# Moving the early input's Hadamard work and the queries' turn to other gaps of an attention pipeline

## Chip, cores and metric

One core of one Trainium2 chip. The metric is the device time of one launch in microseconds (us), as the median of several runs.

## What is computed

The reference is one gated block on 16 sequences of 128 tokens with 512 features, all in fp32:

```python
x = x + tanh(g_xattn[0]) * attention(layernorm(x), ctx, ctx)     # 32 query heads, 8 key/value heads, D = 16
x = x + tanh(g_ffn[0]) * ffn(layernorm(x))

def h_bitlinear(x, w):
    xq = act_quant(fwht(x))          # Hadamard transform, then 8 bits by the row's absolute maximum
    wq = weight_quant(w)             # ternary by the mean absolute weight
    return einsum('bsh,oh->bso', xq, wq)

ffn = h_bitlinear(silu(h_bitlinear(x, w_gate)) * h_bitlinear(x, w_up), w_down)   # 512 -> 2048 -> 512
```

`attention` is a softmax over 128 context positions of the scores divided by 4; keys and values are both the context.

## The kernel before

All 16 sequences (called batches) stay in SBUF. The kernel has two large stages: attention over batches 0 to 15, and then the feed-forward part over four units of four batches. The engines run programs of their own, written out by hand, and meet through counting semaphores; nothing is scheduled for them. What a function such as `step(b)` says for an engine is the order in which that engine works. The change is in the first stage, in `step(b)` of TensorE (`block.tensor`) and of ScalarE (`block.scalar`).

In step b of the attention stage TensorE computes four **quarters**. Quarter (b, j) makes two things side by side: the transposed scores of two groups of heads of batch b (L602 and L627, two PSUM banks, which ScalarE turns into weights with `exp`, L1014), and the *row products* of a quarter seven ahead (L619), that is, scores of batch b+1 or b+2 in the other layout, of which VectorE takes the maxima over the context (`maximum`, L1279, two instructions a quarter). The row products of one quarter go to the two banks that those of the quarter before had, so that they wait for the semaphore `max_done`. Between the quarters lie:

- `weigh(n, kvh)` (L662): the weights times the values of one half of the heads, into bank 6 (`O_BANK`); ScalarE's `copy_out` (L1022) takes it out and counts `oev_done`
- `turn_out(n, kvh)` (L679): that half turned back into rows by tokens, into bank 7 (`T_BANK`); VectorE's `finish` (L1290, L1292) divides by the sums and counts `fin_done`, and GpSimd adds it to x
- `turn_queries(b + 3)` (L716): the normalised queries of a later batch turned, into bank 6; ScalarE's `copy_queries` (L1036) takes them out and counts `qt_done`
- the early input work. The first four batches' attention is complete early, so their input to the feed-forward part is prepared inside the attention stage: `early_turn` in steps 7, 9, 11 and 13 (L725, taken out by `feed_first`, L1110), `early_had` in steps 8, 10, 12 and 14 (L735, the Hadamard product, taken out by `copy_had`, L1072), `early_second` in steps 9, 11, 13 and 15 (L742, taken out at L1104). In the kernel before, all of these use bank 7.

VectorE's `step(b)` is, in this order: the maxima of the first quarter; integers of the early input (L1345, steps 9, 11, 13); batch statistics of batch b+4 (L1264 to L1268, up to step 11); the second quarter's maxima; `finish(b - 1, 0)`; the third quarter's maxima; in steps 8, 10, 12 and 14 `early_peak` (L1327 to L1332, the absolute maximum of the copied Hadamard product); the fourth quarter's maxima; `finish(b - 1, 1)`; `early_round` (L1338); and at the end of steps 5, 7, 9 and 11 the statistics of an early input (L1242 to L1246), ahead of the next step's maxima. GpSimd shifts weights (L466) and works on the early input in between (L491 to L497). Between the second quarter and the third of step b the sign of weights runs on ScalarE (L1052).

In the kernel before, TensorE's row in a step is: quarter 0, `weigh(b-1, 1)`, early turn or early Hadamard product, quarter 1, `turn_out(b-1, 0)`, `turn_queries(b+3)`, quarter 2, `weigh(b, 0)`, `early_second`, quarter 3, `turn_out(b-1, 1)`. Steps 14 and 15 are in `last_steps()`, which the change leaves alone.

## Time and profile before

| | |
|---|---|
| median of 3 runs | 474.78 us (474.51 to 475.0) |
| profiled execution, its time | 474.27 us |
| its span | 472.5 us |
| TensorE busy | 458.6 us |
| VectorE busy | 391.0 us |
| ScalarE busy | 292.8 us |
| GpSimd busy | 211.8 us |

The profile is of one execution. Busy time of TensorE is modelled from pipelined matmuls, which can lie over one another: two matmuls on different rows of the array run side by side and show as two rows that start together. So the table says which engine is loaded, and the timeline, with the starts of the pieces, says where a piece is held.

### The profile page before, as it was taken

The page shows a single profiled execution, that of the slowest core. Times are in us where ns is not written, and L with a number is a line of the kernel's source. Part 1 is how long each engine was busy: PE and PEld are TensorE (multiplying, and loading weights), DVE is VectorE, ACT ScalarE, POOL GpSimd, SP SyncE. Part 2 cuts the span into 40 slices and gives each one's busy share as a digit, 9 for nine tenths or more (in the row PEclk, how much of TensorE's full clock was granted, in tenths as well). Part 3 has the DMA queues.
Part 4 walks back from the last instruction along what each step waited for, and adds up shares of the span by engine and source line. Part 5 has one row for each costly group of instructions (what it writes and reads, how often), then busy time and mean ns, then how long its engine had stood idle before and what let it go on. Part 6 is the DMA issues. An engine that isn't in the chain of part 4 may idle for free.

```text
span 472.5 us, 9016 instructions
## 1 busy us (share of the span) xinstructions
PE 458.6 (97%) x3130; PEld 298.9 (63%) x3130; DVE 391.0 (83%) x745; ACT 292.8 (62%) x465; POOL 211.8 (45%) x314
## 2 busy tenths in 40 slices
PE   8999999999999989999999999999999999999997
PEld 7665656566656534468944469864468874479664
DVE  4889998888977759859998967999895999889892
ACT  4478886667777688877647417643616663647460
POOL 4245455989888464655006734202916300930000
PEclk9999999999999999999999999999999999999999
DMA  7999120121014050000100651100361110153086
GB/s 223 323 348 347 45 53 12 24 58 25 13 22 112 13 166 36 1 1 13 24 11 1 112 135 32 22 11 0 67 141 61 24 24 0 28 92 61 1 140 217
DMA packets 68183, 35.90 MB, mean 76 GB/s; under 512 B 50288, under 2 KB 62960, under 8 KB 68144
## 3 DMA queue, kind: packets, MB, share of 16 engines
q1 hardware_dynamic: 67728, 34.61, 28.8%
q10 hardware_dynamic: 416, 0.79, 0.5%
q8 instruction: 22, 0.36, 0.3%
q14 instruction: 17, 0.14, 0.1%
HBM read 19.26 MB, written 4.19 MB: 50 GB/s over the span
## 4 chain that ended last, share of the span: by engine, by line
PE 70%; DVE 13%; issue 7%; ACT 4%; POOL 2%; DMA 1%; SPq 1%; DVEq 0%; POOLq 0%; ACTq 0%
PE ps L863 15%; PE ps L619 10%; PE ps L917 9%; PE ps L602 8%; PE ps L662 6%; PE ps L940 6%; PE ps L679 3%; PE ps L929 2%; PE ps L931 2%; PE ps L806 2%; DVE wst L1447 2%; ACT wst L1052 2%; DVE y_split L1422 2%; PE ps L716 1%; PE ps L627 1%
## 5 line engine op out<-in xcount | busy, mean ns | idle before, releaser
L863 PE MATMUL ps<-wst 128*128 128x512 bf16 x512 | 113.0, 379 | 2.1 <-DVE wst L1442 2.1
L1279 DVE TENSOR_REDUCE reg<-ps 128x4 f32<-128x512 f32 x128 | 81.9, 684 | 24.7 <-PE ps L619 24.0
L863 PEld LDWEIGHTS ps<-wst 128*128 128x128 bf16 x512 | 49.0, 98 | 62.2 <-DVE wst L1442 4.2
L619 PE MATMUL ps<-reg 32*128 32x256 f32 x512 | 86.7, 400 | 0.9 <-DMA reg<-in_k_t 0.5
L1014 ACT ACTIVATE reg<-ps 128x1024 f32<-128x1024 f32 x64 | 65.6, 1025 | 32.8 <-PE ps L627 32.5
L564 POOL TENSOR_TENSOR reg_rest<-reg_rest,z_sc 128x1024 f32<-128x1024 f32 x24 | 47.3, 2012 | 84.6 <-DVE z_sc L1484 84.6
L1146 ACT ACTIVATE wst<-wst 128x512 f32<-128x512 f32 x64 | 40.0, 627 | 51.8 <-DVE wst L1442 51.5
L917 PE MATMUL ps<-had_f,wst 128*128 128x128 f32 x512 | 67.1, 276 | 1.1 <-DVE wst L1447 1.1
L917 PEld LDWEIGHTS ps<-had_f,wst 128*128 128x128 f32 x512 | 64.1, 191 | 4.4 <-DVE wst L1447 1.8
L602 PE MATMUL ps<-reg 32*128 32x512 f32 x232 | 65.2, 639 | 0.0
L619 PEld LDWEIGHTS ps<-reg 32*128 32x128 f32 x512 | 58.7, 184 | 5.8 <-ACT reg L1036 1.0
L1176 ACT CAST y_split<-ps 128x512 fp32r<-128x512 f32 x64 | 37.4, 585 | 35.8 <-PE ps L917 35.8
L1422 DVE TENSOR_TENSOR y_split<-ps,y_split 128x512 fp32r<-128x512 f32 x64 | 43.4, 683 | 15.0 <-ACT y_split L1176 15.0
L1442 DVE TENSOR_TENSOR wst<-ps,wst 128x512 f32<-128x512 f32 x64 | 43.5, 680 | 8.2 <-PE ps L863 8.2
L1447 DVE TENSOR_TENSOR wst<-ps,wst 128x512 f32<-128x512 f32 x64 | 43.4, 678 | 1.4 <-ACT wst L1146 1.3
L940 PE MATMUL ps<-wst,reg_rest 128*128 128x512 bf16 x192 | 42.8, 380 | 0.0
L1185 ACT COPY reg_rest<-ps 128x512 f32<-128x512 f32 x64 | 37.8, 591 | 2.1 <-PE ps L931 2.1
L459 POOL TENSOR_TENSOR x_all<-x_all,reg 128x256 f32<-128x256 f32 x32 | 23.9, 746 | 32.9 <-DVE reg L1292 32.8
L1461 DVE TENSOR_REDUCE mz<-reg_rest 128x8 f32<-128x1024 f32 (+1 forms) x33 | 38.3, 1171 | 0.0
L940 PEld LDWEIGHTS ps<-wst,reg_rest 128*128 128x128 bf16 x192 | 27.4, 144 | 13.9 <-issue 0.5
L662 PE MATMUL ps<-reg 128*32 128x512 f32 x256 | 34.1, 605 | 0.1
L929 PE MATMUL ps<-y_split,had_r 128*128 128x512 f32 x64 | 30.6, 478 | 0.0
(168 smaller groups left out, 738.1 us busy)
## 6 DMA issues: line engine op xcount, KB each, us to landing
wst<-in_w SPq DMA_DIRECT2D x16, 512.0 KB, 8.6
reg<-in_w SPq DMA_DIRECT2D x8, 512.0 KB, 5.6
out<-x_all SPq DMA_DIRECT2D x16, 256.0 KB, 2.1
x_all<-in_x SPq DMA_DIRECT2D x3, 1024.0 KB, 9.5
reg<-in_k_t SPq DMA_DIRECT2D x32, 32.0 KB, 2.4
reg<-in_v SPq DMA_DIRECT2D x4, 256.0 KB, 4.1
x_all<-in_x ACTq DMA_DIRECT2D x1, 512.0 KB, 4.8
reg_rest<-reg SPq DMA_TRANSPOSE x20, 3.0
```

The lines of the kernel that those rows point to most:

```text
L564: pool.tensor_tensor(z, z, sc, ALU.mult).then_inc(sem("z_scaled"), 1)
L602: pe.matmul(ps[:, bank + m, :], kpad[b // CHUNK % 2][strip(i), b % CHUNK, a, :], q_t[b % 4][strip(i), :], start=True, stop=False)
L619: last = pe.matmul(ps[:, row_banks(r) + m, 256 * g:256 * g + 256], q_t[n % 4][strip(i), P * h:P * h + P], kpad[n // CHUNK % 2][strip(i), n ...
L662: last = pe.matmul(O_BANK[SLOT * l:SLOT * l + SLOT, :], v_pad[n // CHUNK % 2][:, n % CHUNK, 4 * kvh + l, :], probs[:, 4 * kvh + l, :], sta ...
L863: last = pe.matmul(ps[:, banks[ob % n], :], tern_gu[:, ob // 2, m, j, P * (ob % 2):P * (ob % 2) + P], q1_t[:, j, :], start=(j == 0), stop= ...
L917: last = pe.matmul(ps[:, Y_BANKS[s % 3], P * k:P * k + P], X[:, 4 * s + k, :, :].rearrange("p c t -> p (c t)"), had_f[:, :], start=True, s ...
L940: last = pe.matmul(ps[:, bank, :], q2.rearrange("p g (t c) -> p c (g t)", c=NC)[:, c, P * tb:P * tb + P], tern_d[:, c, :], start=(c == 0), ...
L1014: act.activation(probs[:, 2 * j:2 * j + 2, :], ps[:, bank:bank + 2, :], ACT.Exp, scale=D ** -0.5).then_inc(sem("exp_done"), 1)
L1279: dve.tensor_reduce(neg_max[n % 2][:, g:g + 2, i + m, :], ps[:, row_banks(r) + m, :].rearrange("p (g a t) -> p g a t", g=2, a=2), AX_X, AL ...
L1422: dve.tensor_tensor(y_low[s % RING], ps[:, Y_BANKS[s % 3], :], y_high[s % RING].bitcast(F32), ALU.subtract).then_inc(sem("y_low"), 1)
L1442: dve.tensor_tensor(gs[ob % GS], ps[:, G_BANKS[ob % 2], :], s_row, ALU.mult).then_inc(sem("gs_done"), 1)
L1447: dve.tensor_tensor(X[:, :, ob, :], ps[:, U_BANKS[ob % 3], :].rearrange("p (g t) -> p g t", g=NG), gs[ob % GS].rearrange("p (g t) -> p g t ...
```

## The change

In steps 7 to 13 (`EARLY`) the early turn or the early Hadamard product moves from behind quarter 0 to behind quarter 1 and `turn_out(b-1, 0)`, and goes into bank 6 instead of bank 7. Bank 6 is free there only when `copy_out(b-1, 1)` is through (`oev_done`), and `weigh(b, 0)`, which writes bank 6 next, waits for ScalarE's copy. The queries' turn, which has bank 6 too, moves from its place behind quarter 1 to the end of the step, behind quarter 3 and `turn_out(b-1, 1)`; it waits for `copy_out(b, 0)`, and `weigh(b, 1)` waits for its copy. ScalarE's copies are moved in the same way. In step 14 the Hadamard product keeps its place and bank. The orders of VectorE, GpSimd and the DMA queues are the same.

```diff
--- before.py
+++ after.py
@@ -236,12 +236,17 @@
         FIRST_DMA = 5
         SECOND_UNIT = {13: (0, 1), 15: (2, 3)}
         FRONTS = {5: 0, 7: 1, 9: 2, 11: 3}
+        EARLY = range(7, 14)
         G_PLACE = 5
         ROUND_ACT = {9: 0, 11: 1}
         G_BANKS = (0, 2)
         U_BANKS = (1, 3, 6)
         T_BANK = ps[:, 7, :]
         O_BANK = ps[:, 6, :]
+
+        def had_bank(b):
+
+            return O_BANK if b in EARLY else T_BANK
 
         block = ctx.enter_context(nc.Block())
 
@@ -652,7 +657,11 @@
                     pe.wait_ge(sem("v_set"), n // CHUNK + 1)
                 pe.wait_ge(sem("exp_done"), QUARTERS * n + 2 * kvh + 2)
                 reach(pe, sem("oev_done"), 2 * n + kvh)
-                if kvh == 0 and exists(n + 3):
+                if kvh == 0 and n in EARLY_HAD and n in EARLY:
+                    pe.wait_ge(sem("f_hc"), EARLY_HAD[n] + 1)
+                if kvh == 0 and n in EARLY_TURN:
+                    pe.wait_ge(sem("f_xt"), EARLY_TURN[n] + 1)
+                if kvh == (1 if n in EARLY else 0) and exists(n + 3):
                     pe.wait_ge(sem("qt_done"), n + 4)
                 if kvh == 1 and n + 1 < FIRST_DMA:
                     pe.wait_ge(sem("mt_done"), n + 2)
@@ -669,12 +678,10 @@
                     return
                 pe.wait_ge(sem("oev_done"), 2 * n + kvh + 1)
                 reach(pe, sem("fin_done"), 2 * n + kvh)
-                if kvh == 0 and n + 1 in EARLY_HAD:
+                if kvh == 0 and n + 1 in EARLY_HAD and n + 1 not in EARLY:
                     pe.wait_ge(sem("f_hc"), EARLY_HAD[n + 1] + 1)
                 if kvh == 1 and n + 1 in EARLY_SECOND:
                     pe.wait_ge(sem("f_sg"), EARLY_SECOND[n + 1] + 1)
-                if kvh == 0 and n + 1 in EARLY_TURN:
-                    pe.wait_ge(sem("f_xt"), EARLY_TURN[n + 1] + 1)
                 for g in range(G):
                     last = pe.transpose(T_BANK[:, P * g:P * g + P], o_t[kvh][:, P * g:P * g + P], ident_f[:, :])
                 last.then_inc(sem("to_done"), 1)
@@ -711,7 +718,7 @@
                 elif n == 2:
                     pe.wait_ge(sem("qt_done"), 2)
                 elif n > 3:
-                    pe.wait_ge(sem("oev_done"), 2 * (n - 3))
+                    pe.wait_ge(sem("oev_done"), 2 * (n - 3) + (1 if n - 3 in EARLY else 0))
                 for j in range(NJ):
                     last = pe.transpose(O_BANK[:, P * j:P * j + P], q_norm[n % 2][:, P * j:P * j + P], ident_f[:, :])
                 last.then_inc(sem("tq_done"), 1)
@@ -720,9 +727,9 @@
 
                 tb = EARLY_TURN[b]
                 pe.wait_ge(sem("f_b2"), 2 * tb + 2)
-                pe.wait_ge(sem("fin_done"), 2 * b - 2)
+                pe.wait_ge(sem("oev_done"), 2 * b)
                 for j in range(NJ):
-                    last = pe.transpose(T_BANK[:, P * j:P * j + P], xn_first[tb][:, P * j:P * j + P], ident_f[:, :])
+                    last = pe.transpose(O_BANK[:, P * j:P * j + P], xn_first[tb][:, P * j:P * j + P], ident_f[:, :])
                 last.then_inc(sem("f_t1"), 1)
 
             def early_had(b):
@@ -730,9 +737,12 @@
                 if tb == 0:
                     pe.wait_ge(sem("const_in"), 16 * 5)
                 pe.wait_ge(sem("f_xt"), tb + 1)
-                pe.wait_ge(sem("fin_done"), 2 * b - 2)
+                if b in EARLY:
+                    pe.wait_ge(sem("oev_done"), 2 * b)
+                else:
+                    pe.wait_ge(sem("fin_done"), 2 * b - 2)
                 for j in range(NJ):
-                    last = pe.matmul(T_BANK[:, P * j:P * j + P], xn_t[:, P * j:P * j + P], had_f[:, :], start=True, stop=True)
+                    last = pe.matmul(had_bank(b)[:, P * j:P * j + P], xn_t[:, P * j:P * j + P], had_f[:, :], start=True, stop=True)
                 last.then_inc(sem("f_h"), 1)
 
             def early_second(b):
@@ -771,19 +781,22 @@
             def step(b):
                 quarter(b, 0)
                 weigh(b - 1, 1)
+                quarter(b, 1)
+                turn_out(b - 1, 0)
                 if b in EARLY_HAD:
                     early_had(b)
                 if b in EARLY_TURN:
                     early_turn(b)
-                quarter(b, 1)
-                turn_out(b - 1, 0)
-                turn_queries(b + 3)
+                if b not in EARLY:
+                    turn_queries(b + 3)
                 quarter(b, 2)
                 weigh(b, 0)
                 if b in EARLY_SECOND:
                     early_second(b)
                 quarter(b, 3)
                 turn_out(b - 1, 1)
+                if b in EARLY:
+                    turn_queries(b + 3)
                 turn_max(b + 1)
 
             def down_sum():
@@ -1066,20 +1079,24 @@
                 act.wait_ge(sem("const_in"), 16 * 5)
                 act.copy(had16_r.rearrange("p (t c) -> p c t", c=NC), xn_t[:, 0:P].rearrange("p (c t) -> p c t", c=NC)).then_inc(sem("had16_set"), 1)
 
-            def copy_had(tb):
+            def copy_had(b):
+                tb = EARLY_HAD[b]
                 act.wait_ge(sem("f_h"), tb + 1)
                 reach(act, sem("f_qf"), tb)
-                act.copy(had_out, T_BANK).then_inc(sem("f_hc"), 1)
+                act.copy(had_out, had_bank(b)).then_inc(sem("f_hc"), 1)
 
             def step(b):
                 exp(b, 0)
                 copy_out(b - 1, 1)
-                if b in EARLY_HAD:
-                    copy_had(EARLY_HAD[b])
+                if b in EARLY_HAD and b not in EARLY:
+                    copy_had(b)
+                exp(b, 1)
+                if b in EARLY_HAD and b in EARLY:
+                    copy_had(b)
                 if b in EARLY_TURN:
                     feed_first(EARLY_TURN[b])
-                exp(b, 1)
-                copy_queries(b + 3)
+                if b not in EARLY:
+                    copy_queries(b + 3)
                 halves = ABS_ACT.get(b, ())
                 for h in halves[0:1]:
                     absolute(h)
@@ -1090,6 +1107,8 @@
                 if b in EARLY_SECOND:
                     feed_second(EARLY_SECOND[b])
                 exp(b, 3)
+                if b in EARLY:
+                    copy_queries(b + 3)
                 copy_max(b + 1)
                 for h in halves[1:]:
                     absolute(h)
@@ -1107,7 +1126,7 @@
                 act.wait_ge(sem("f_t1"), tb + 1)
                 reach(act, sem("f_h"), tb)
                 act.wait_ge(sem("had16_set"), 1)
-                act.copy(xn_t, T_BANK).then_inc(sem("f_xt"), 1)
+                act.copy(xn_t, O_BANK).then_inc(sem("f_xt"), 1)
 
             act.wait_ge(sem("mhalf_set"), 3)
             normalise_q(0)
```

TensorE's row in step 8, from the end of quarter 0. L602, L619 and L627 are a quarter, L662 weighs, L735 is the Hadamard product, L679 `turn_out`, L716 `turn_queries`. Before:

```order
L627 MATMUL ps<-reg 128x512 x2
L662 MATMUL ps<-reg 32x512 x4
L735 MATMUL ps<-had_f,wst 128x128 x4
L602 MATMUL ps<-reg 128x512 x2
L619 MATMUL ps<-reg 128x256 x4
L627 MATMUL ps<-reg 128x512 x2
L679 MATMUL ps<-ident_f,reg 128x128 x4
L716 MATMUL ps<-ident_f,reg 128x128 x4
L602 MATMUL ps<-reg 128x512 x2
```

After (L607, L624, L632 are a quarter, L671 weighs, L745 is the Hadamard product, L686 `turn_out`):

```order
L632 MATMUL ps<-reg 128x512 x2
L671 MATMUL ps<-reg 32x512 x4
L607 MATMUL ps<-reg 128x512 x2
L624 MATMUL ps<-reg 128x256 x4
L632 MATMUL ps<-reg 128x512 x2
L686 MATMUL ps<-ident_f,reg 128x128 x4
L745 MATMUL ps<-had_f,wst 128x128 x4
L607 MATMUL ps<-reg 128x512 x2
```

The Hadamard product has gone from behind the weighing to behind `turn_out`, where the queries' turn stood; between quarters 0 and 1 only the weighing is left.

The same engine from quarter 3 of step 8 to the first matmuls of step 9, before:

```order
L602 MATMUL ps<-reg 128x512 x2
L619 MATMUL ps<-reg 128x256 x4
L627 MATMUL ps<-reg 128x512 x2
L679 MATMUL ps<-ident_f,reg 128x128 x4
L602 MATMUL ps<-reg 128x512 x2
```

After (L723 is `turn_queries`):

```order
L607 MATMUL ps<-reg 128x512 x2
L624 MATMUL ps<-reg 128x256 x4
L632 MATMUL ps<-reg 128x512 x2
L686 MATMUL ps<-ident_f,reg 128x128 x4
L723 MATMUL ps<-ident_f,reg 128x128 x4
L607 MATMUL ps<-reg 128x512 x2
```

The queries' turn now stands between quarter 3 and the next step's quarter 0.

ScalarE in step 8, from the exponential of quarter 0 on: L1014 is an exponential, L1022 `copy_out`, L1072 `copy_had`, L1036 `copy_queries`, L1052 a sign of weights. Before (the first row also holds the last exponential of step 7):

```order
L1014 ACTIVATE reg<-ps 128x1024 x2
L1022 COPY reg<-ps 128x512
L1072 COPY wst<-ps 128x512
L1014 ACTIVATE reg<-ps 128x1024
L1036 COPY reg<-ps 128x512
L1052 ACTIVATE wst<-wst,magics 128x1024
L1014 ACTIVATE reg<-ps 128x1024
L1022 COPY reg<-ps 128x512
L1014 ACTIVATE reg<-ps 128x1024
```

After (L1027 an exponential, L1035 `copy_out`, L1086 `copy_had`, L1065 a sign, L1049 `copy_queries`):

```order
L1027 ACTIVATE reg<-ps 128x1024
L1035 COPY reg<-ps 128x512
L1027 ACTIVATE reg<-ps 128x1024
L1086 COPY wst<-ps 128x512
L1065 ACTIVATE wst<-wst,magics 128x1024
L1027 ACTIVATE reg<-ps 128x1024
L1035 COPY reg<-ps 128x512
L1027 ACTIVATE reg<-ps 128x1024
L1049 COPY reg<-ps 128x512
```

The copy of the Hadamard product goes behind the second exponential, and the queries' copy behind the fourth.

## Rows read from the trace of the kernel before

**Rows 1.** The page's first part, TensorE: busy us (share of the span), instructions.
```profile
PE 458.6 (97%) x3130; PEld 298.9 (63%) x3130; DVE 391.0 (83%) x745; ACT 292.8 (62%) x465; POOL 211.8 (45%) x314
```

**Rows 2.** Timeline of TensorE, batch 12: start us, us, instruction, count.
```profile
137.28 0.66 PE L679 MATMUL ps<-ident_f,reg 128*128 128x128 f32 x4
...
137.87 0.70 PE L602 MATMUL ps<-reg 32*128 32x512 f32 x2
...
139.62 1.07 PE L662 MATMUL ps<-reg 128*32 128x512 f32 x8
...
140.61 1.16 PE L735 MATMUL ps<-had_f,wst 128*128 128x128 f32 x8
...
141.70 0.70 PE L602 MATMUL ps<-reg 32*128 32x512 f32 x2
...
142.97 0.66 PE L679 MATMUL ps<-ident_f,reg 128*128 128x128 f32 x4
...
144.00 0.70 PE L602 MATMUL ps<-reg 32*128 32x512 f32 x2
...
145.38 1.06 PE L662 MATMUL ps<-reg 128*32 128x512 f32 x8
...
147.65 0.66 PE L679 MATMUL ps<-ident_f,reg 128*128 128x128 f32 x4
```

**Rows 3.** Timeline of VectorE, batch 12, its maxima; idle time before them in brackets.
```profile
137.22 1.29 DVE L1279 TENSOR_REDUCE reg<-ps 128x4 f32<-128x512 f32 x2 [1.50 <-PE ps L619]
...
140.18 1.28 DVE L1279 TENSOR_REDUCE reg<-ps 128x4 f32<-128x512 f32 x2
...
142.98 1.29 DVE L1279 TENSOR_REDUCE reg<-ps 128x4 f32<-128x512 f32 x2 [1.52 <-PE ps L619]
...
145.21 1.29 DVE L1279 TENSOR_REDUCE reg<-ps 128x4 f32<-128x512 f32 x2 [0.26 <-PE ps L619]
```

**Rows 4.** Timeline of TensorE and then of VectorE, batch 6.
```profile
78.34 1.07 PE L662 MATMUL ps<-reg 128*32 128x512 f32 x8
...
81.30 0.66 PE L679 MATMUL ps<-ident_f,reg 128*128 128x128 f32 x4
...
78.91 1.28 DVE L1279 TENSOR_REDUCE reg<-ps 128x4 f32<-128x512 f32 x2
80.11 0.68 DVE L1264 BATCH_NORM_STATS2 st<-x_all 128x6 f32<-128x512 f32 x1
...
81.12 1.29 DVE L1279 TENSOR_REDUCE reg<-ps 128x4 f32<-128x512 f32 x2
```

**Rows 5.** Timeline of TensorE and then of VectorE, batch 13.
```profile
149.98 1.06 PE L662 MATMUL ps<-reg 128*32 128x512 f32 x8
...
152.84 0.66 PE L679 MATMUL ps<-ident_f,reg 128*128 128x128 f32 x4
...
155.24 1.06 PE L662 MATMUL ps<-reg 128*32 128x512 f32 x8
...
157.93 0.66 PE L679 MATMUL ps<-ident_f,reg 128*128 128x128 f32 x4
...
149.93 1.27 DVE L1279 TENSOR_REDUCE reg<-ps 128x4 f32<-128x512 f32 x2
151.13 0.41 DVE L1345 TENSOR_SCALAR q_b<-wst 128x512 bf16<-128x512 f32 x1
...
152.84 1.29 DVE L1279 TENSOR_REDUCE reg<-ps 128x4 f32<-128x512 f32 x2 [1.30 <-PE ps L619]
```

**Rows 6.** Timeline of VectorE, batch 11, the first quarter's maxima.
```profile
129.41 1.27 DVE L1279 TENSOR_REDUCE reg<-ps 128x4 f32<-128x512 f32 x2
```

**Rows 7.** Timeline of ScalarE, batch 12, the copy of the Hadamard product.
```profile
141.81 0.59 ACT L1072 COPY wst<-ps 128x512 f32<-128x512 f32 x1 [0.47 <-PE ps L735]
```

**Rows 8.** Timeline of VectorE and then of GpSimd, end of batch 10.
```profile
126.60 0.45 DVE L1332 TENSOR_SCALAR f_max<-wsc,f_max 128x2 f32<-128x2 f32 x1
...
125.90 1.12 POOL L466 TENSOR_SCALAR wst<-wst,w_inv 128x1024 f32<-128x1024 f32 x1
```

## The prediction

> **What bounds the kernel now.** The page's first part comes first: TensorE is busy for 97% of the span [rows 1]. That share alone says little here, since a matmul that waits in a queue behind a semaphore does not show as idle. So I read next the timeline of TensorE in one batch of the stage that the change touches, batch 12 [rows 2], and beside it VectorE's maxima [rows 3]. In the rows I take as the end of a quarter the start of what follows it on TensorE, since TensorE works in order.
>
> The reader is to see how long each piece takes. The second quarter runs from 141.70 to 142.97, 1.27 us. The first runs from 137.87 to 139.62, 1.75 us, and the third from 144.00 to 145.38, 1.38 us. All three hold the same matmuls, so 0.48 us of the first and 0.11 of the third are waiting. The wait is for VectorE: a quarter's row products (L619) may not write their two banks before the two maxima (L1279) of the quarter before have read them. The maxima of the fourth quarter begin at 137.22 and the next quarter ends at 139.62, 2.40 later; those of the second begin at 142.98 and the third ends at 145.38, again 2.40 later [rows 2, 3]. In batch 6 they begin at 78.91 and the quarter ends at 81.30, 2.39 later [rows 4]; in batch 13 from 152.84 to 155.24, 2.40 [rows 5]. So this stage has one rule, in numbers of this trace: **a quarter ends at the later of (its start + 1.27) and (start of the former quarter's maxima + 2.40)**. What TensorE does between two quarters is free up to about 1.1 us, and dear beyond it.
>
> The other durations: weighing 0.99 (139.62 to 140.61), the Hadamard product 1.09 (140.61 to 141.70), turning a half of the output 0.59 (137.28 to 137.87), and with the queries' turn 1.03 (142.97 to 144.00), so the queries' turn is 0.44 [rows 2]. The early input's turn (L725) lies in batch 13 between 149.98 and 152.84 with a weighing and a quarter: 2.86 - 0.99 - 1.27 = 0.60 [rows 5].
>
> **The change, part by part.** No operation is added or removed; bank 6 stands in for bank 7 and two pieces of TensorE's row change place. Seen from TensorE alone this fills gaps: the queries' turn goes to where 0.48 us are waited, the early work away from where weighing already fills 0.99. What it is worth is decided by when VectorE starts its maxima, and VectorE's own order is not touched.
>
> *The queries' turn before the first quarter.* In batch 12's place the first quarter would start at 137.28 + 1.03 = 138.31 and end at 139.58 unhindered; the maxima give 137.22 + 2.40 = 139.62. It ends at 139.62, as now. The 0.44 us are hidden in the wait, but nothing comes earlier.
>
> *Even batches 8, 10, 12 (Hadamard product).* Behind the first quarter only the weighing is left, so the second could start at 140.61 and end at 141.88. But VectorE starts the first quarter's maxima only at 140.18, because in batches 7, 9 and 11 the statistics of an early input (L1242 to L1246) stand ahead of them. 140.18 + 2.40 = 142.58. Batch 6 shows this very case, for the statistics of batch 5 stand ahead of it and it has no early work between its first two quarters: its second quarter begins after 78.34 + 0.99 = 79.33 and ends at 81.30, 1.97 us, a wait of 0.70 [rows 4]. So the second quarter comes 0.39 earlier than now (142.97), not 1.09. Then follow 0.59 + 1.09 and the third quarter: 142.58 + 1.68 + 1.27 = 145.53, against 145.38 now. The second quarter's maxima don't bind it: even where batch statistics follow the first maxima (batches 8 and 10), VectorE is free at 140.18 + 1.20 + 1.01 = 142.39, and 2.40 more is 144.79. (1.20 from 78.91 to 80.11, 1.01 from 80.11 to 81.12 [rows 4].) The third quarter's maxima start 1.21 after it, as from 144.00 to 145.21 [rows 2, 3]: 144.26 + 1.21 = 145.47, and the fourth ends at the later of 145.53 + 0.99 + 1.27 = 147.79 and 145.47 + 2.40 = 147.87. Now it ends at 147.65. **A Hadamard batch gets 0.22 us longer**: the product now lies where it is no longer a cover for VectorE's lateness. Three of them: +0.66.
>
> *Batch 13 (turn, last one).* First quarter at 149.98 as now; its maxima start at 149.93, so the second ends at 149.93 + 2.40 = 152.33 (unhindered 152.24) against 152.84. Then 0.59 + 0.60 + 1.27 gives 154.79 (VectorE's integers, 0.41 from 151.13, are done long before and do not bind). From there to the batch's end 2.69 as now (155.24 to 157.93), 157.48: 0.45 shorter [rows 5].
>
> *Batches 9 and 11.* They have batch statistics as well. In batch 11 the first maxima start at 129.41 [rows 6], so the second quarter ends at 131.81, and VectorE comes to the second maxima at 129.41 + 1.20 + 0.41 + 1.01 = 132.03. The third quarter: unhindered 131.81 + 0.59 + 0.60 + 1.27 = 134.27, by the maxima 134.43; plus 2.69 is 137.12, against 137.28 [rows 2]. 0.16 shorter each, 0.32 for both. Batch 7 has no Hadamard batch ahead and the weights' scales on VectorE; I take 0.1, between nothing and batch 11's 0.16.
>
> *New waits, costed at nothing.* Weighing (b, 0) now waits for ScalarE's copy out of bank 6. In batch 12 the product would end at 142.58 + 0.59 + 1.09 = 144.26; the copy starts 0.11 behind it (141.70 to 141.81) and takes 0.59 [rows 7], so it is done at 144.96, and the weighing is due at 145.53: 0.57 us of cover. After the turn in batch 13 the cover is the same to 0.02. The queries' copy is done 1.03 + 0.11 + 0.59 = 1.73 behind the fourth quarter, the weighing (b, 1) due 2.34 behind it: 0.61 of cover. If a cover were gone, its batch would lose what is missing; behind these copies on ScalarE stand a sign or an exponential, whose result TensorE asks for two quarters later.
>
> The sum: +0.66 - 0.45 - 0.32 - 0.10 = **-0.21 us**. The profiled execution took 474.27 (span 472.5), and 474.06 would follow; its time lies 0.51 below the median of the runs, 474.78, and I put the same difference against that: 474.6. Behind batch 13 everything moves along, and batches 14 and 15 are as they were.
>
> **The rivals.** Measurement tells 0.2%, 0.95 us, from no change.
> - *TensorE's gaps count in full.* If the maxima followed TensorE at once, the queries' turn would save 1.75 - 1.38 = 0.37 in front of six batches, and the early work 0.11 in six third quarters and 155.24 - 152.84 - 0.59 - 1.27 = 0.54 in batch 13: 2.22 + 0.66 + 0.54 = 3.4 us, 471.4. For it speaks that each of these gaps is in the rows; against it batch 6, and that the first quarter's maxima at 140.18 don't depend on TensorE. 8 in 100. A share of it, over 0.95, because VectorE comes to its maxima earlier in most batches: 473.5, 6 in 100.
> - *Even batches break even.* If only their 0.66 were wrong, the result is -0.87, 473.9, still no change that can be told: 8 in 100.
> - *VectorE is held by GpSimd.* Ahead of the fourth quarter's maxima in a Hadamard batch stands a small product (L1332). In batch 10 it runs from 126.60 to 127.05 while GpSimd shifts weights from 125.90 to 127.02 [rows 8]: it ends when that does, and the maxima behind it, on which the next batch's first quarter depends, come late. The change moves VectorE against GpSimd. If it now meets the start of such an instruction it is held for its whole 1.12 us instead of 0.45, 0.67 a batch; with its neighbour L1338 held likewise twice that. Three batches give 2.0 to 4.0, less 0.2: 476.6 to 478.6. It decides from (0.95 + 0.21) / 3 = 0.39 a batch. GpSimd's order follows VectorE's though, and the moves are of 0.2 us. 6 in 100.
> - *A new wait binds.* Were ScalarE late by 0.57 plus 0.2 in each of seven batches (a sign ahead of the copy would do it, and none stands there), +1.2 net, 476.0. 3 in 100.
>
> The Trainium skill's page "SBUF — State Buffer" (section "Who interferes with whom") says that VectorE and GpSimd share one port pair as an exclusive lock, which a scalar product out of SBUF can take and which a reduction never needs. The trace agrees for L1332, which ended 0.03 from the end of GpSimd's instruction; no row here shows maxima held. By that rule the sum stays and only the third rival lives.
>
> **How the numbers follow.** Forecast 0.69, its own range 474.0 to 475.1, from 0.05 to 0.1 of error in each of seven batches. With "even batches break even" 0.77 lie within 0.2%; faster 0.14 (0.08 + 0.06); slower 0.09 (0.06 + 0.03). The range, which may leave out 2 in 10, goes to 473.7 below and 475.5 above.
>
> **What the changed profile would show.** Right: between the end of the fourth quarter and the end of the next first quarter still 2.34 us; a second quarter of about 1.97 us in batches 8, 10 and 12; third quarters of 1.27 in the even batches; the batches' lengths up by 0.2 in the even ones and down by 0.1 to 0.5 in the odd ones; no wait of the weighing on ScalarE's copies. Wrong: second quarters of 1.3 us in the even batches (first rival), the small product L1332 longer than 0.5 us (third), or the weighing starting over 0.1 behind the third quarter's last matmul (fourth).

## The result: faster, and by far more than forecast

The changed kernel takes 472.91 us (median of 6 runs, 472.81 to 473.67) against 474.70 us for the kernel before (6 runs, 474.29 to 475.0). The ratio is 0.9968 with a 95% interval of 0.9957 to 0.9978. That is a gain of 1.0 to 2.0 us where 0.2 was forecast, and outside the range. Its profiled execution took 472.94 us, 1.33 less than that of before. The kernel before took 474.36 to 474.46 us (medians of 7 to 21 executions) beside the later experiments, so the gain may well be nearer to 1.5 us than to the 1.8 between the two medians above. One execution of e6 ran at a granted clock of 0.982 (481.89 us) and is left out of its ratio; all others of the experiments ran at 0.999 or 1.000.

The page's head and first part, after:

```profile
span 471.1 us, 8996 instructions
## 1 busy us (share of the span) xinstructions
PE 455.3 (97%) x3110; PEld 299.1 (63%) x3130; DVE 390.4 (83%) x745; ACT 292.2 (62%) x465; POOL 211.2 (45%) x314
```

The span is 1.4 us shorter (472.5 before). TensorE's share of it is the 97% of [rows 1]: waits in its queue don't show as idle. The stretches that follow are batches 7 to 13, each from the end of its predecessor's fourth quarter to the end of its own, by the starts of `turn_out` on TensorE. Columns: stretch and its length, then busy time and count of TensorE, its weight loads, VectorE, ScalarE and GpSimd, the granted clock (1.00 is the 2.4 GHz level), DMA share and GB/s. Before:

```profile
85.93:95.73 9.80, 9.80 (x93) 6.04 (x91) 7.94 (x19) 6.63 (x9) 8.96 (x17) 1.00 0.06 13
95.73:106.09 10.36, 10.36 (x95) 6.48 (x93) 9.24 (x22) 7.23 (x9) 8.06 (x15) 1.00 0.26 66
106.09:116.49 10.40, 10.40 (x93) 6.18 (x91) 8.38 (x19) 8.40 (x11) 9.81 (x18) 1.00 0.14 28
116.49:126.86 10.37, 10.37 (x95) 6.48 (x93) 9.26 (x22) 7.22 (x9) 8.52 (x16) 1.00 0.06 13
126.86:137.28 10.42, 10.42 (x93) 6.21 (x90) 8.39 (x19) 8.40 (x11) 9.83 (x19) 1.00 0.12 27
137.28:147.65 10.37, 10.37 (x95) 6.48 (x93) 8.32 (x20) 7.23 (x9) 8.07 (x15) 1.00 0.43 115
147.65:157.93 10.28, 10.28 (x90) 5.99 (x87) 7.08 (x15) 7.98 (x10) 8.19 (x14) 1.00 0.13 27
```

After:

```profile
86.09:95.54 9.45, 9.45 (x88) 5.96 (x86) 7.82 (x19) 6.06 (x8) 8.61 (x17) 1.00 0.06 14
95.54:105.85 10.31, 10.31 (x94) 6.59 (x92) 9.07 (x22) 7.21 (x9) 8.28 (x15) 1.00 0.25 66
105.85:116.01 10.16, 10.16 (x92) 6.28 (x90) 8.26 (x19) 8.33 (x11) 9.56 (x18) 1.00 0.14 29
116.01:126.39 10.38, 10.38 (x94) 6.63 (x92) 9.13 (x22) 7.22 (x9) 8.71 (x16) 1.00 0.06 13
126.39:136.56 10.17, 10.17 (x93) 6.28 (x91) 8.27 (x19) 8.33 (x11) 9.58 (x19) 1.00 0.13 27
136.56:146.94 10.38, 10.38 (x95) 6.63 (x93) 8.28 (x20) 7.22 (x9) 8.88 (x16) 1.00 0.48 115
146.94:156.59 9.65, 9.65 (x92) 5.89 (x90) 7.12 (x15) 8.17 (x11) 7.51 (x13) 1.00 0.13 29
```

| batch | 7 | 8 | 9 | 10 | 11 | 12 | 13 | sum |
|---|---|---|---|---|---|---|---|---|
| forecast | -0.10 | +0.22 | -0.16 | +0.22 | -0.16 | +0.22 | -0.45 | -0.21 |
| measured | -0.35 | -0.05 | -0.24 | +0.01 | -0.25 | +0.01 | -0.63 | -1.50 |

The whole gain lies in these seven batches. (In the execution of after, batch 7 begins 0.16 us later, and what follows passes the gain on: 1.34 at the end of batch 13, 1.4 in the span.) Every batch is better than forecast. The three with the Hadamard product miss by 0.21 to 0.27 each, 0.69 together, and the four others by 0.60. TensorE's timeline of batch 12, after, beside [rows 2]:

```profile
136.56 0.66 PE L686 MATMUL ps<-ident_f,reg 128*128 128x128 f32 x4
...
137.58 0.70 PE L607 MATMUL ps<-reg 32*128 32x512 f32 x2
...
138.89 1.06 PE L671 MATMUL ps<-reg 128*32 128x512 f32 x8
...
139.89 0.70 PE L607 MATMUL ps<-reg 32*128 32x512 f32 x2
...
141.85 0.66 PE L686 MATMUL ps<-ident_f,reg 128*128 128x128 f32 x4
...
142.34 1.06 PE L745 MATMUL ps<-had_f,wst 128*128 128x128 f32 x8
...
143.33 0.70 PE L607 MATMUL ps<-reg 32*128 32x512 f32 x2
...
144.60 1.07 PE L671 MATMUL ps<-reg 128*32 128x512 f32 x8
...
146.94 0.66 PE L686 MATMUL ps<-ident_f,reg 128*128 128x128 f32 x4
```

And VectorE's maxima of the fourth quarter of batch 11 and the first of batch 12, beside [rows 3]:

```profile
136.49 1.29 DVE L1298 TENSOR_REDUCE reg<-ps 128x4 f32<-128x512 f32 x2 [1.69 <-PE ps L624]
...
139.46 1.28 DVE L1298 TENSOR_REDUCE reg<-ps 128x4 f32<-128x512 f32 x2
```

The first quarter ends 138.89 - 136.56 = 2.33 behind the batch's start, as forecast (2.34). The first maxima begin 2.90 behind it, as before, and the second quarter ends at 141.85, 5.29 behind (forecast 5.30), 2.39 behind the start of those maxima: it takes 1.96 us, 0.69 of them waiting. So far each number is the forecast's. Then `turn_out` and the Hadamard product take 143.33 - 141.85 = **1.48** us. The forecast had added 0.59 and 1.09, 1.68, from their durations in [rows 2]. `turn_out` starts 0.49 ahead of the product, and the product 0.99 ahead of the quarter. That 0.20 is what the batch misses.

### The profile page after: what moved, and what is told of

It is laid out like the page before. It is cut to its first block, busy times and chain, and to the rows that moved or that the text cites. A ratio compares the mean times of both kernels' runs of the same rounds, so it can differ in the third digit from the quotient of the medians.

```text
span 471.1 us, 8996 instructions
## 1 busy us (share of the span) xinstructions
PE 455.3 (97%) x3110; PEld 299.1 (63%) x3130; DVE 390.4 (83%) x745; ACT 292.2 (62%) x465; POOL 211.2 (45%) x314
## 4 chain that ended last, share of the span: by engine, by line
PE 70%; DVE 13%; issue 8%; ACT 4%; POOL 2%; DMA 1%; SPq 1%; DVEq 0%; POOLq 0%; ACTq 0%
PE ps L876 15%; PE ps L624 10%; PE ps L930 9%; PE ps L607 7%; PE ps L671 6%; PE ps L953 6%; PE ps L686 4%; PE ps L942 2%; PE ps L944 2%; PE ps L819 2%; DVE wst L1466 2%; DVE y_split L1441 2%; ACT wst L1065 2%; PE ps L632 2%; PE ps L723 1%
## 5 line engine op out<-in xcount | busy, mean ns | idle before, releaser
L876 PE MATMUL ps<-wst 128*128 128x512 bf16 x499 | 111.7, 379 | 3.3 <-DVE wst L1461 2.1
L624 PE MATMUL ps<-reg 32*128 32x256 f32 x512 | 87.0, 399 | 1.2 <-DMA reg<-in_k_t 0.7
L1027 ACT ACTIVATE reg<-ps 128x1024 f32<-128x1024 f32 x64 | 65.5, 1024 | 32.0 <-PE ps L632 31.8
L607 PE MATMUL ps<-reg 32*128 32x512 f32 x232 | 65.2, 639 | 0.0
L624 PEld LDWEIGHTS ps<-reg 32*128 32x128 f32 x512 | 59.2, 184 | 6.2 <-ACT reg L1049 1.3
L671 PE MATMUL ps<-reg 128*32 128x512 f32 x256 | 34.1, 605 | 0.1
L607 PEld LDWEIGHTS ps<-reg 32*128 32x128 f32 x232 | 17.5, 183 | 24.9 <-issue 23.5
```

Of the source, the lines that this page charges most:

```text
L607: pe.matmul(ps[:, bank + m, :], kpad[b // CHUNK % 2][strip(i), b % CHUNK, a, :], q_t[b % 4][strip(i), :], start=True, stop=False)
L624: last = pe.matmul(ps[:, row_banks(r) + m, 256 * g:256 * g + 256], q_t[n % 4][strip(i), P * h:P * h + P], kpad[n // CHUNK % 2][strip(i), n ...
L671: last = pe.matmul(O_BANK[SLOT * l:SLOT * l + SLOT, :], v_pad[n // CHUNK % 2][:, n % CHUNK, 4 * kvh + l, :], probs[:, 4 * kvh + l, :], sta ...
L876: last = pe.matmul(ps[:, banks[ob % n], :], tern_gu[:, ob // 2, m, j, P * (ob % 2):P * (ob % 2) + P], q1_t[:, j, :], start=(j == 0), stop= ...
L1027: act.activation(probs[:, 2 * j:2 * j + 2, :], ps[:, bank:bank + 2, :], ACT.Exp, scale=D ** -0.5).then_inc(sem("exp_done"), 1)
```

## The experiments

**Theory.** TensorE works in blocks: quarters and weighings use 32-row or 32-column tiles of its array (32\*128, 128\*32 in the rows), transposes and Hadamard products the full 128\*128. A block of full-array matmuls between tiled ones costs some 0.15 to 0.20 us beyond its matmuls, once. Four transposes add 0.43 to 0.44, four products 0.89. In the kernel before, the early work was a block of its own; now it shares one with `turn_out`. **Rival theory:** the pieces are shorter at the new place for another reason (bank, neighbours that are lighter). A second question is what holds VectorE in front of the maxima.

### e1: the change in the odd batches only

```diff
-        EARLY = range(7, 14)
+        EARLY = (7, 9, 11, 13)
...
                 weigh(b - 1, 1)
+                if b in EARLY_HAD and b not in EARLY:
+                    early_had(b)
```

> The change only in the odd batches 7, 9, 11 and 13; batches 8, 10 and 12 keep the Hadamard product behind the weighing, in bank 7, and the queries' turn behind the second quarter. By the prediction's sum (a moved Hadamard product costs 0.22 us a batch) this must be 0.66 us faster than the changed kernel: 472.3, even batches of 10.37 us as before the change. By the theory formed on the trace of after (a block of full-array matmuls that joins another saves the 0.20 us which it costs to stand alone, which pays for the 0.22) the even batches are worth nothing either way: 472.9, and again batches of 10.3 to 10.4 us.

Measured 473.08 us, ratio to before 0.9973 (0.9963 to 0.9983), against 0.9968 for the full change. Batches 8, 10 and 12 are 10.32, 10.36 and 10.36 us, batches 9, 11 and 13 10.14, 10.20 and 9.70, as in after. The prediction's sum would have had 472.3, a ratio of 0.995, which lies outside the interval. So in even batches the change is worth nothing either way: what VectorE's lateness costs without its cover (0.22) is what the shared block gives back (0.20).

### e2: a small tiled matmul between `turn_out` and the early work

```diff
                 turn_out(b - 1, 0)
+                if b in EARLY:
+                    pe.wait_ge(sem("oev_done"), 2 * b)
+                    pe.matmul(O_BANK[:, 0:8], kpad[b // CHUNK % 2][strip(0), b % CHUNK, 0, :],
+                              q_t[b % 4][strip(0), 0:8], start=True, stop=True)
                 if b in EARLY_HAD:
                     early_had(b)
```

> The changed kernel with one tiny matmul on a 32-row tile (8 columns, its result is overwritten) between turn_out and the early work in batches 7 to 13, so that the early work no longer follows full-array matmuls directly. In after, turn_out and the product take 1.48 us in batch 12 (from 141.85 to 143.33), turn_out and the early turn 1.02. Theory 'each change between tiled and full-array matmuls costs about 0.1 us': 1.68 or more and 1.2 or more, even batches 10.5 to 10.6 us instead of 10.3 to 10.4. Rival 'the pieces are shorter because of the other bank or the other place': 1.50 and 1.05, batches unchanged.

TensorE in batch 12 of this kernel (L686 `turn_out`, L788 the small matmul, L745 the product):

```profile
143.76 0.66 PE L686 MATMUL ps<-ident_f,reg 128*128 128x128 f32 x4
144.35 0.38 PE L788 MATMUL ps<-reg 32*128 32x8 f32 x2
144.66 1.16 PE L745 MATMUL ps<-had_f,wst 128*128 128x128 f32 x8
145.75 0.70 PE L607 MATMUL ps<-reg 32*128 32x512 f32 x2
```

`turn_out` is back at 0.59 and the product at 1.09 (144.66 to 145.75), the very durations that they have apart in the kernel before, though bank and place are the new ones. The small matmul takes 0.31 itself, so the even batches take 10.83 to 10.88 us, more than the 10.5 to 10.6 expected. The kernel took 475.66 us in one run. The rival theory falls: bank and place are those of the changed kernel. A small full-array matmul in the same place was not run, so e2 alone leaves open whether any matmul between would do it. But in the changed kernel transposes with other weights and another bank stand directly ahead of the product, and the 0.20 is gone; so neither a change of weights nor one of bank costs it.

### e7: the Hadamard product twice, in the kernel before

```diff
-                for j in range(NJ):
+                for j in [*range(NJ), *range(NJ)]:
                     last = pe.matmul(T_BANK[:, P * j:P * j + P], xn_t
```

> The kernel before with the early Hadamard product issued twice in a row at its old place (same operands, same result). Alone it takes 1.09 us between a weighing and a quarter. Theory 'a block of full-array matmuls costs about 0.2 us for standing alone, and the product 0.89': the two take 1.98 us. Rival 'the product takes 1.09 at this place': 2.18.

```profile
99.21 2.05 PE L735 MATMUL ps<-had_f,wst 128*128 128x128 f32 x16
101.19 0.70 PE L602 MATMUL ps<-reg 32*128 32x512 f32 x2
```

16 instead of 8 rows, and 1.98 us: the second product cost 0.89. With 1.09 for the first, standing alone costs 0.20. (477.57 us, one run.)

The traces also say at which end of a block it is paid. In the changed kernel `turn_out` takes 0.59 us ahead of a quarter and 0.49 ahead of another full-array piece: 0.10 for leaving. The product takes 1.09 behind a weighing and 0.99 behind `turn_out`, 0.10 for entering; the early turn takes 0.59 and 0.53, 0.06 for entering. Weighings and quarters don't pay: in every order that was run an unhindered quarter takes 1.27 to 1.28 us and a weighing 0.99 to 1.00, whatever stands beside them. But a weighing (128\*32) and a quarter (32\*128) always alternate with each other or with full-array pieces, so what a change between these two tiled forms costs was not seen.

### e6: only the queries' turn moved

```diff
                 turn_out(b - 1, 0)
-                turn_queries(b + 3)
+                if b not in EARLY:
+                    turn_queries(b + 3)
...
                 turn_out(b - 1, 1)
+                if b in EARLY:
+                    turn_queries(b + 3)
```

The waits for bank 6 and ScalarE's copy move with it, as in the change.

> The kernel before with only the queries' turn moved to the end of steps 7 to 13; the early work stays behind the weighing in bank 7. By the rule that a quarter ends no earlier than 2.40 us behind the start of the former quarter's maxima, the queries' turn was hidden in neither place: the third quarters and the first quarters both end where they did, batches stay 10.36 to 10.42 us, 474.5. By the rival 'TensorE's gaps count in full' the first quarters shrink by 0.37 us in six batches: 472.3.

474.35 us, ratio 0.9998 (0.9989 to 1.0008). In batch 10 the third quarter starts 0.44 us earlier, behind `turn_out` alone:

```profile
121.90 0.66 PE L680 MATMUL ps<-ident_f,reg 128*128 128x128 f32 x4
122.49 0.70 PE L603 MATMUL ps<-reg 32*128 32x512 f32 x2
...
124.30 1.07 PE L663 MATMUL ps<-reg 128*32 128x512 f32 x8
```

It still ends 2.40 behind the start of the second quarter's maxima (121.90 on VectorE, L1286). The rule on the maxima holds in both places, and the rival "TensorE's gaps count in full" is out.

### e3 and e4: the early input's statistics at another place of VectorE's order

```diff
                 maximum(b + 2, 1)
+                if b in FRONTS:
+                    reach(dve, sem("f_ap"), FRONTS[b])
+                    statistics(Index(None, FRONTS[b]), ("f_bn", "f_mv", "f_ve"), 2)
...
-                if b in FRONTS:
-                    reach(dve, sem("f_ap"), FRONTS[b])
-                    statistics(Index(None, FRONTS[b]), ("f_bn", "f_mv", "f_ve"), 2)
```

e3 does this in the changed kernel, e4 in the one before.

> The changed kernel with the early input's statistics on VectorE (end of steps 5, 7, 9, 11) done between the third and fourth quarter's maxima of the same step instead of ahead of the next step's first maxima. Theory 'in even batches the second quarter waits 0.70 us for maxima that these statistics make late': the second quarters of batches 6, 8, 10 and 12 fall from 1.95 to 1.3 us, batch 6 gets 0.56 shorter, 8, 10 and 12 about 0.6 each, 2.4 in all, 470.5 us. Rival 'TensorE waits there for something else (ScalarE's exponential, GpSimd's maxima)': nothing, 472.9. If the statistics only make the fourth quarter's maxima late instead, odd batches get up to 1 us longer and the time is 472.5 to 473.5.

> The same move of the statistics in the kernel before the change. If the early Hadamard product behind the first weighing covers VectorE's lateness, as the prediction has it, only batch 6 gains, 0.56 us: 474.1. If the lateness costs time there as well, batches 8, 10 and 12 gain too, up to 2 us, 472.7.

**e3** took 471.36 us, ratio 0.9936 (0.992 to 0.9953); once more beside e9 (below), 471.54 and 0.9937. The second quarter of batch 10 is down from 1.96 to 1.30 us, on TensorE:

```profile
118.76 0.70 PE L607 MATMUL ps<-reg 32*128 32x512 f32 x2
...
120.06 0.66 PE L686 MATMUL ps<-ident_f,reg 128*128 128x128 f32 x4
```

Batches 8, 10 and 12 are 9.71 us each, 0.60 to 0.67 shorter, and batch 6 went from 9.92 to 9.27. That is 2.6 us, where 2.4 were expected. But batches 7, 9, 11 and 13 got longer, 9.78, 10.41, 10.48 and 9.83, 1.07 us together, which the expectation had not counted. GpSimd's shift of weights (L471), VectorE's product of scales (L1351) and the maxima behind it, in batch 8 of e3:

```profile
104.25 1.13 POOL L471 TENSOR_SCALAR wst<-wst,w_inv 128x1024 f32<-128x1024 f32 x1
...
104.81 0.59 DVE L1351 TENSOR_SCALAR f_max<-wsc,f_max 128x2 f32<-128x2 f32 x1
...
105.30 1.27 DVE L1298 TENSOR_REDUCE reg<-ps 128x4 f32<-128x512 f32 x2
```

A product of two columns takes 0.59 us and ends at 105.40; GpSimd's instruction ends at 105.38. The maxima begin 0.28 behind the end of the fourth quarter (105.02) instead of ahead of it. In batch 8 of each of these kernels the product ends within 0.03 us of a GpSimd instruction's end: 0.42 us in the kernel before, 0.35 in after, 0.59 in e3, 0.76 in e4, where it came behind the start of the instruction after the shift, L491, and waited for that one. From after to e3 the products ahead of batches 9, 11 and 13 got longer by 0.24, 0.31 and 0.18 us, and in batch 7 the product of the weights' scales (L1377, also 128x2) went from 0.36 to 0.63: 1.00 of the 1.07. **e4** took 474.53 us, ratio 0.9999 (0.9989 to 1.0009), not the 474.1 expected: batch 6 gained 0.64, and batches 9 and 11 lost 0.35 and 0.33, ahead of which the products took 0.34 and 0.30 us longer. The even ones stayed at 10.36 us, so the old place of the product did cover the statistics, as the prediction said.

### e5 and e8: the product of scales behind the maxima

```diff
-                dve.tensor_scalar(f_max[:, 4:6], wsc[:, 0:2], f_max[:, 1:2], C_E, ALU.mult, ALU.mult
-                                  ).then_inc(sem("f_c"), 1)
             def early_round(tb):
-                dve.wait_ge(sem("f_c"), 4 * tb + 4)
+                dve.wait_ge(sem("f_c"), 4 * tb + 3)
+                dve.tensor_scalar(f_max[:, 4:6], wsc[:, 0:2], f_max[:, 1:2], C_E, ALU.mult, ALU.mult
+                                  ).then_inc(sem("f_c"), 1)
```

e5 is this on e3, e8 on the changed kernel.

> The kernel of e3 with VectorE's small product of scales (L1351, 128x2) moved from ahead of the fourth quarter's maxima to behind them and behind finish, at the start of early_round. In e3 it ran 0.59 and 0.66 us in batches 8 and 10, each time until GpSimd's shift of weights ended, and batches 9 and 11 were 10.41 and 10.48 us instead of the 10.16 of after. Theory 'VectorE was held by GpSimd in front of the maxima on which the next first quarter waits': the maxima begin at the end of the fourth quarter again, batches 9, 11 and 13 get 0.2 to 0.3 us shorter each, 470.7. Rival 'odd batches are longer because the statistics now stand between the third and fourth quarter's maxima': no change, 471.4.

> The changed kernel with only the small product of scales moved behind the fourth quarter's maxima. In after it ran 0.35 us in batches 8 and 10 and ended with GpSimd's shift of weights, and the maxima began 0.04 us behind the end of the fourth quarter, 0.10 later than they could. Theory of the port: up to 0.1 us in two batches, 472.8, which a time can't tell from none but the profile can: the maxima of the fourth quarter of batches 8 and 10 begin 0.05 ahead of its end. Rival: the maxima are late because of the peak's own reduction, and nothing moves.

Both expectations failed. e5 took 471.88 us (0.9946, 0.9932 to 0.9959), not 470.7, and e8 474.27 (0.9998, 0.9989 to 1.0008), 1.4 over after where at most 0.1 was at stake. The maxima of the fourth quarter do begin on time. But the product now meets the next GpSimd instruction and holds back `early_round` (L1357), which then meets the one after. Batch 8 into 9 of e5, L501 and L502 being GpSimd's butterflies:

```profile
106.48 0.78 DVE L1355 TENSOR_SCALAR f_max<-wsc,f_max 128x2 f32<-128x2 f32 x1
...
106.51 0.73 POOL L501 TENSOR_TENSOR wst<-wst 128x256 f32<-128x256 f32 x1
...
107.17 1.03 DVE L1357 TENSOR_SCALAR wst<-wst,f_max 128x512 f32<-128x512 f32 x1
...
107.19 0.74 POOL L502 TENSOR_TENSOR wst<-wst 128x256 f32<-128x256 f32 x1
...
108.13 1.27 DVE L1298 TENSOR_REDUCE reg<-ps 128x4 f32<-128x512 f32 x2
```

The next first maxima, at 108.13, are 3.40 behind the end of the batch (104.73), against 2.50 in after. Batch 9 is 11.03 us in e5, and batches 9 and 11 are 10.82 each in e8, 0.65 over after. So the mechanism was right and the place wrong: held instructions line up.

### e9 and e11: the product of scales on ScalarE

```diff
+            def scales_act(tb):
+                act.wait_ge(sem("wsce_done"), 1)
+                act.wait_ge(sem("f_c"), 4 * tb + 3)
+                act.activation(f_max[:, 4:6], wsc_e[:, :], ACT.Copy, scale=f_max[:, 1:2]).then_inc(sem("f_c"), 1)
```

Both are built on e3. ScalarE calls this behind the queries' copy, and VectorE's product is taken out of `early_peak`. In e9 VectorE makes `wsc_e` (the weights' scales times a constant) in batch 7, in e11 ScalarE does in batch 8.

> The kernel of e3 with the small product of scales off VectorE: ScalarE makes it behind the queries' copy (one copy with a scale, from the weights' scales times a constant, which VectorE makes once in batch 7). Nothing of two columns stands ahead of the fourth quarter's maxima, or ahead of early_round as in e5. Theory of the port: maxima of the fourth quarter at its end minus 0.05 in batches 8, 10 and 12, and early_round, if it meets no GpSimd instruction, 0.5 to 0.6 us: batches 9 and 11 of about 10.1 to 10.2 us instead of 10.4 and 10.5, 470.7. If early_round itself is held (1.0 us, as in e5), nothing is won over e3, 471.4 to 471.9.

> The kernel of e3 once more, beside e9 on the same chip, so that the two can be compared: 471.4, 3.0 us under the kernel before.

> The kernel of e9 with the weights' scales times the constant also made by ScalarE, in batch 8. In e9 VectorE made them in batch 7 ahead of the first maxima, which began 1.40 us behind the statistics of the weights instead of 0.94 in e3, and batch 7 was 10.25 us instead of 9.78, while batches 9 and 11 were 9.87. Theory: every small product out of SBUF ahead of maxima can be held by GpSimd, so batch 7 gets 0.4 to 0.5 us shorter, 470.7. Rival: batch 7 was longer for another reason, 471.15.

e9 took 471.15 us (0.993, 0.9916 to 0.9944), where 470.7 was expected; its interval overlaps that of e3 beside it, so the batches have to tell the two apart. The maxima of batch 8's fourth quarter and `early_round` (L1364):

```profile
105.42 1.29 DVE L1306 TENSOR_REDUCE reg<-ps 128x4 f32<-128x512 f32 x2
...
107.31 0.48 DVE L1364 TENSOR_SCALAR wst<-wst,f_max 128x512 f32<-128x512 f32 x1
```

The end of batch 8 lies at 105.55, so the maxima are on time, and `early_round` takes 0.48. Batches 9, 11 and 13 fell to 9.87, 9.88 and 9.65 (10.1 to 10.2 was expected of the first two). Batch 7 rose to 10.25, and in e11, without VectorE's extra product, it is 9.75: **470.39 us**, ratio to before 0.9911 (0.9894 to 0.9927), the fastest kernel of the study, 2.5 us under the changed one.

## Why the prediction was wrong, step by step

- **"A quarter ends at the later of (its start + 1.27) and (start of the former quarter's maxima + 2.40)"**: right. It gives every quarter of batch 12 after to 0.02, and e6.
- **The queries' turn before the first quarter is free and brings nothing earlier**: right (2.33 against 2.34; e6).
- **Even batches: the second quarter comes only 0.39 earlier, since the statistics make the first maxima late**: right (5.29 against 5.30 behind the batch's start; e3 took the 0.66 away).
- **"Then follow 0.59 + 1.09 and the third quarter"**: this is the step that failed, and with it "Then 0.59 + 0.60 + 1.27" of batch 13. The sum took over the durations that the pieces have standing apart. Side by side they take 1.48 and 1.02 (batch 7: 90.91 to 91.93; batch 13: 151.57 to 152.59). In even batches that is 0.20 each, 0.60 in all; in batch 7 it is 0.17; in batch 13, where the second quarter's maxima (151.51 + 2.40) then end the third quarter, 0.12 of the 0.17 count. In batches 9 and 11 it is worth nothing, since there the maxima end the third quarter, as forecast. [Rows 2] had it: `turn_out` takes 0.59 alone, and the queries' turn behind it, of the same four transposes, adds 0.44. I read this as the queries' price and gave the early turn, which is the same work, 0.60.
- **Batch 7, 0.1 by analogy**: mis-sized. Its first maxima begin at 88.47 in the kernel before, so the second quarter would end at 90.87, the third start at 90.87 + 0.59 + 0.60 = 92.06 and its maxima at 93.27, and the batch end at 95.67: 0.06 before 95.73. With the shared block it is 0.23, and 0.10 more came from VectorE's product of the weights' scales (0.47 us before, 0.36 after).
- **Batches 9 and 11**: 0.16 forecast, 0.24 and 0.25 measured. The product of scales ahead of them was held 0.07 and 0.10 us less, by which the first maxima begin 0.03 and 0.05 earlier behind the batch's start. The other 0.04 is a term of the sum: it took the integers (L1345) at their row's 0.41, but in batch 11 of the kernel before they run from 130.61 and the statistics behind them start at 130.98, 0.37.
- Sum: -0.21 - 0.89 for the shared blocks (0.60 + 0.17 + 0.12) = -1.10; the remaining 0.40 of -1.50 are such small shifts of VectorE against GpSimd, the 0.04, and roundings.
- **New waits costed at nothing**: right; in batches 7 to 13 each copy out of bank 6 was done at least 0.5 us before the weighing behind it (batch 12: 144.02, weighing 144.60).
- **The rival "Even batches break even" (8 in 100)**: this is what the even batches did (-0.05, +0.01, +0.01), but the prediction gave no reason for it. Its 473.9 was still too slow, for the other four batches missed by 0.60 as well.
- **The rival "VectorE is held by GpSimd"**: did not decide here (in after the product was held a little less, not more) but is real, and its price of 0.67 us a batch was about right: in e8 one product of two columns, moved, made batches 9 and 11 longer by 0.65 each and the kernel by 1.4 us.

The Trainium skill's page "TensorEngine Tiling (Array Packing)", section "Key Properties", says that a change of tiling mode, not just of tile, drains TensorE. That agrees with e2 and e7, and it is the rule that spoke against my sum; the page gives no time for it. The runs give 0.20 for a Hadamard product, 0.15 to 0.16 for four transposes, for the changes at both ends of a block. No row shows a drain itself. The weight loads fit too. Before, the load for the product starts with it:

```profile
140.61 0.97 PEld L735 LDWEIGHTS ps<-had_f,wst 128*128 128x128 f32 x8 [0.84 <-issue]
```

After, it starts 0.10 ahead of the first matmul (142.34), behind transposes of the same shape:

```profile
142.24 0.97 PEld L745 LDWEIGHTS ps<-had_f,wst 128*128 128x128 f32 x8
```

The 0.10 by which the load leads is as much as the product saves at its entering end. What the 0.10 at the leaving end is, and how much of either is a drain or a load that nothing covers, was not separated.

## What to carry to other kernels

Don't price a moved TensorE piece by its duration where it stands now. Price its matmuls, and then count how many changes between tiled and full-array matmuls the new order has; one block fewer was worth 0.12 to 0.20 us a batch here where TensorE set the pace of the next quarter, and nothing in batches 9 and 11, where VectorE did. And where one engine's order has a late point (statistics ahead of maxima), moving the other engine's work around it trades cover against gaps to no gain (e1, even batches); moving the late work itself brought 2.6 us in the batches that had waited, and cost 1.1 in the others (e3), most of which came back with the small product on ScalarE (e11).

## What was not expected of the hardware

- The switch between tiled and full-array matmuls, above.
- A VectorE product of 128x2 out of SBUF takes 0.21 us at best here (batch 12 of after, between two GpSimd instructions), up to 0.78 in the batches above (e5), and 1.03 to 1.04 in batch 14 of the kernels that have it there, the one before included (165.99 to 167.03, with GpSimd's shift from 165.88 to 167.01). It ends with the GpSimd instruction that is under way. `early_round` on 128x512 took 0.48 and up to 1.04 (e8). The maxima, reductions out of PSUM, took 1.26 to 1.29 a pair throughout. A VectorE instruction on one column out of SBUF (L1348, 128x1) took its 0.15 in the middle of the same shift of weights (105.37 in after, shift from 104.83 to 105.96). The page "SBUF — State Buffer" (section "Who interferes with whom") of the Trainium skill names the shared port pair for this; these runs agree. GpSimd pays in turn: in e9 its butterfly (L502 there, from 107.34) took 1.03 us instead of 0.73 where `early_round` had started 0.03 ahead of it. Which of the two pays can't be read from the starts of the rows alone: in e5 the product's row also starts 0.03 ahead of GpSimd's (106.48 and 106.51), and there the product was the one held.
